# A graph kernel on one core: each selection of the gather stages moved from ahead of its neighbour's lift to the head of its own slot

## The reference, cut to what matters

```python
mean = jax.ops.segment_sum(h, dst, N) / degc
mean_sq = jax.ops.segment_sum(h * h, dst, N) / degc
std = jnp.sqrt(jax.nn.relu(mean_sq - mean * mean) + EPS_VAR)
mx = jax.ops.segment_max(h, dst, N)
mn = jax.ops.segment_min(h, dst, N)
...
out = jnp.concatenate([x, out], axis=-1) @ W_post + b_post
return out @ W_lin + b_lin
```

## Time and profile before

| what | us |
| --- | --- |
| median of 3 runs | 2146.79 |
| lowest and highest of them | 2123.44, 2160.79 |
| the profiled execution's own time | 2106.36 |
| its span, first to last instruction | 2104.6 |
| gather stage of layer 0 in the span | about 636 to 1250 |
| gather stage of layer 1 in the span | about 1362 to 1982 |
| TensorE's mean granted clock | 0.863 |

### The profile page before, as it was taken

The page is one execution under the profiler, slowest core; times in us unless marked ns, Lnnn a source line. Parts: engine busy times, 40 slices in busy tenths (PEclk is TensorE's granted clock), DMA queues, the critical chain, the costliest instruction groups (busy, mean ns, idle before and its releaser), DMA issues.

```text
span 2104.6 us, 30157 instructions
## 1 busy us (share of the span) xinstructions
PE 1443.8 (69%) x11250; PEld 1041.9 (50%) x11250; DVE 1423.3 (68%) x2879; ACT 502.3 (24%) x1074; POOL 804.5 (38%) x831
## 2 busy tenths in 40 slices
PE   0267777666974777877777865636777887787564
PEld 0156777655972444545554542424444554455432
DVE  7899999783425866666666754766655776676457
ACT  3357777500112111111111110310111111111101
POOL 4400000014006455556655624065545555565230
PEclk9879888886996988989988987978888998898876
DMA  5323333322443555555656532344555565565320
GB/s 119 94 110 140 140 140 140 125 87 93 161 139 98 178 171 192 178 186 184 200 167 197 184 113 63 92 141 161 176 181 176 187 201 182 170 219 170 139 63 25
DMA packets 126252, 309.57 MB, mean 147 GB/s; under 512 B 21744, under 2 KB 73408, under 8 KB 125742
## 3 DMA queue, kind: packets, MB, share of 16 engines
q1 hardware_dynamic: 75216, 145.00, 19.7%
q10 hardware_dynamic: 23470, 105.20, 14.2%
q0 software_dynamic: 27440, 57.77, 10.0%
HBM read 167.18 MB, written 140.75 MB: 146 GB/s over the span
## 4 chain that ended last, share of the span: by engine, by line
DVE 34%; PE 32%; issue 14%; another core or an unknown queue 12%; DMA 3%; ACT 2%; POOL 2%; ACTq 1%; DVEq 0%; POOLq 0%
PE ps L1190 16%; PE ps L1305 6%; DVE accs L2246 5%; DVE scanned L2275 4%; DVE accs L2228 4%; DVE scanned L1769 3%; DVE scanned L1766 3%; DVE scanned L1775 3%; PE ps L1317 2%; PE ps L1215 2%; PE ps L1405 1%; DVE S L1742 1%; DMA A<-counts 1%; ACT Y L756 1%
## 5 line engine op out<-in xcount | busy, mean ns | idle before, releaser
L1129 POOL DMA_INDIRECT scanned<-table,rest_idx x688 | 675.2, 981 | 712.1 <-DMA rest_history<-scanned 248.1
L1190 PE MATMUL ps<-big,A 125*128 125x128 bf16 (+1 forms) x7500 | 756.0, 257 | 60.9 <-issue 49.4
L1190 PEld LDWEIGHTS ps<-big,A 125*128 125x128 bf16 x7500 | 622.9, 103 | 190.9 <-issue 83.4
L1305 PE MATMUL ps<-S,big 126*128 126x500 bf16 (+1 forms) x1050 | 276.2, 406 | 251.7 <-DVE accs L2246 171.0
L2246 DVE TENSOR_TENSOR accs<-accs,ps 128x1000 f32<-128x1000 f32 (+1 forms) x154 | 166.7, 1083 | 342.7 <-remote 257.1
L2275 DVE SCALAR_TENSOR_TENSOR scanned<-scanned,rest_neg 128x256 f32<-128x256 f32 x688 | 331.7, 482 | 40.6 <-issue 7.6
L1305 PEld LDWEIGHTS ps<-S,big 126*128 126x128 bf16 x1050 | 101.1, 106 | 371.3 <-DVE accs L2246 187.5
L1215 PE MATMUL ps<-scanned 128*128 128x150 bf16 x1050 | 115.6, 252 | 76.3 <-DVE scanned L1775 75.4
L2228 DVE TENSOR_TENSOR accs<-accs,ps 128x1000 f32<-128x1000 f32 (+1 forms) x154 | 165.9, 1077 | 1.8 <-DVE sums_t L1883 1.3
L1148 POOL IOTA Y<- 128x784 int32 x1 | 0.8, 786 | 359.9 <-DVEq L2033 359.9
L1215 PEld LDWEIGHTS ps<-scanned 128*128 128x128 bf16 x1050 | 87.2, 132 | 92.7 <-issue 71.2
(11 more groups left out here) (395 smaller groups left out, 1410.0 us busy)
## 6 DMA issues: line engine op xcount, KB each, us to landing
rest_history<-scanned SPq DMA_DIRECT2D x172, 512.0 KB
A<-counts ACTq DMA_DIRECT2D x75, 800.0 KB
S<-picks SPq DMA_DIRECT2D x60, 640.0 KB
picks<-S ACTq DMA_DIRECT2D x25, 800.0 KB
counts<-A ACTq DMA_DIRECT2D x25, 800.0 KB
scanned<-table,rest_idx POOLq DMA_INDIRECT x688
table<-Y SPq DMA_DIRECT2D x10, 320.0 KB, 2.6
S<-picks SPq DMA_DIRECT2D x10, 160.0 KB
```

What stands on the lines that cost most here:

```text
L1129: nc.gpsimd.indirect_dma_start(out=lanes[:, r, s, 0:F], out_offset=None, in_=tables[1 + l], in_offset=bass.IndirectOffsetOnAxis(ap=rest_id ...
L1190: m = nc.tensor.matmul(acc[:, bank, 0:width], A[0:NB, slot, a, :], XS[0:NB, a, c, 0:width], start=a == 0 and c == 0, stop=a == NT - 1 and ...
L1305: m = nc.tensor.matmul(ps[:, bank + h, 0:len(blocks) * NB], XS[0:NB + 1, a, c, 0:F], pick[0:NB + 1, part % RING, 0:len(blocks), a % PART, ...
```

## The change

The selection of a slot is issued at the head of that slot. Before, the first one was issued ahead of the loop, and in each slot the next slot's selection was issued ahead of the lift of the current one.

```diff
-                select(l, 0)
                 for s in range(NSLOT):
-                    if s + 1 < NSLOT:
-                        select(l, s + 1)
+                    select(l, s)
                     fold(s)
                     if s - 2 in AT_FRONT:
                         use_operands(l, AT_FRONT[s - 2])
```

## The result

Timed side by side on one chip, the changed kernel took 2163.32 us (median of 4 runs, 2155.39 to 2175.61) and the kernel before 2135.11 us (4 runs, 2110.9 to 2160.79): a ratio of 1.022, with a 95% interval of 1.013 to 1.032. Executions of one kernel spread by a few per cent, and every ratio here leaves out those over 1.5% above the fastest of their kernel, while the medians are over all runs, so a ratio is not the quotient of the two medians beside it (1.013 here). The profiled execution after took 2155.39 us, with a span of 2153.6 us and a mean granted clock of 0.854; before it was 2106.36, 2104.6 and 0.863.

A forecast was written before the change was run, and what follows sets the result against it. No engine was taken as full; the gather stages wait for late TensorE signals. Terms of +2 (clean slots), +12 (after late signals) and -2 (slots 0 to 5) sum to +12 us: 2146.79 becomes 2159 us, range 2106 to 2177.

The forecast's parts named there:

- The wait at the selection: TensorE's idle before the selections that `take_low` ended, 171.0 us, should fall to near nothing.
- rival A: Wait at the selection is a true limit; the chain restarts sooner after late signals: -87 us, 2060 us, chance 0.15.
- The chain inside a slot: Selection start to lift takes 2.72 us, bare by 0.13 or 0.30 us; at most 19.6 us for both layers.
- How many slots pay it: Of 96 slots up to 86 follow a late signal; the ten left pay 0.2 us each, +2 us.
- After a late signal: The next lift comes 0.27 us later after each of 43 late signals, at the low clock: +12 us.
- Where the signals strike: `take_low` should still wait some 40 times for "remote", near 257 us; such waits before `take_top` would contradict this.
- B: Rival: late signals strike the selection too, 1.9 us each, 82 us on top of 12: 2241 us, chance 0.20.
- slots 77 to 90: In slots 78 to 90 the pieces ahead cover a selection and maximum of 125 columns: 0.
- Slots 0 to 5: The lift no longer stands behind a selection waiting for a `take_low`: -1 us a layer.
- The clock: The low clock should last about as long as before; a mean well over 0.863 would speak for a sooner restart.

The follow-up runs named there:

- e1: The kernel before, with the next slot's selection moved from ahead of the current slot's lift to directly behind it: 2131.62 us, ratio 0.987.
- the quiet pair: The kernels before and after, each with three quarters of the row gathers left out: 1787.39 and 1811.77 us, 24.4 us apart.
- e2: The changed kernel, unedited, measured again beside the kernel before: 2167.8 us, ratio 1.004.
- e11: The changed kernel, unedited, measured once more in more rounds beside the kernel before: 2155.0 us, ratio 1.015.
- e10: The changed kernel, with each row gather waiting until the row 14 ahead of it was scanned: 2105.24 us, ratio 0.990 to the kernel before.
- e5_before_quarter_timed: The kernel before with one of four row gathers issued, the other rows scanned as zeros: 1787.39 us, ratio 0.836.

## Why the prediction was right, and where its steps were not

The forecast was 2159 us, 12 above the median, in a range of 2106 to 2177, and a change within 2% was given 0.65. Measured were 2163 us, and +28, +13 and +38 us by the medians of three comparisons, or about +48, +9 and +32 by their ratios: some 30 on the average. The sign held and the range held. The size of the change did not, being over twice the 12, and neither did its split into terms. That 2163 lies 4 us from 2159 is luck: the forecast started from a median of 2146.79 for the kernel before, and beside the changed one it took 2135.11.

**The wait at the selection.** It was to be near nothing, and is (8.4 us of idle in the groups, none of it ended by `take_low`). Behind it there was no 87 us to be had: e1 takes the same wait away without the change's price and gains 24 us, and nothing with the gathers paced. This is rival A at its most.

**The chain inside a slot.** 2.72 us from the start of the selection to the lift, bare by 0.13 us in F and 0.30 in T: measured 2.73 us, 0.15 and 0.31 to 0.33, and 0 in U by the median step. In the pair without late signals, slots 9 to 77 cost 18.2 us where the sum with all slots clean said 19.6. Each duration was in the rows of before, and adding them in the order of their dependence gave the chain's length. That 18.2 is so near 19.6 holds for the sum only: by kinds it is 0.3 in F, 12.8 in T and 5.0 in U, where the prediction had 7.0, 12.6 and 0.

**How many slots pay it.** This is the step that failed, and it failed twice. I took ten of 96 and +2 us, because two slots follow each of 43 late signals. But of those 86 slots many are U slots, lie outside 9 to 77, or follow two late signals: in the trace of before only 53 are F or T slots of 9 to 77, so 43 were left, some +9 us by the prediction's own rule. And the slots behind a late signal do pay. In the three profiles of the kernel after, 51, 60 and 49 F and T slots come one or two behind a wait of over 2 us for a late signal, and in 31, 35 and 29 of them the maximum starts within 0.1 us of the selection's end and the lift within 0.1 us of the maximum's: the chain is bare there too. The times fit: 24.4 us where no signal is late, some 30 on the average where 43 and more are.

**After a late signal.** +0.27 each, 12 us. It can't be read alone. If the other terms are as in the quiet pair, (9 - 24.4) / 43 = -0.36 to (48 - 24.4) / 43 = +0.55 us is left for each, in which a gain and a loss behind a late signal may cancel. A net gain of 2.03 us each (a sooner restart at the full clock) doesn't go with this, nor one of 0.95. Rival A falls with the times: the changed kernel was faster in no comparison.

**Where the signals strike.** `take_low` was to go on waiting for "remote" about 40 times, 257 us. It did 19 times, 62.7 us; 39 times and 209.7 us stand before `take_top`. By the prediction's own test that makes B right, since 77% of the wait moved. Late signals do strike the selection, but the price of 82 us on top is not there: the kernel took 2163 us and not 2241, and the late signals' waits sum to 326, 324 and 326 us in the three profiles after, 36 more than the 290 before. There is one place where the price is seen. In slots 77 to 90, where the prediction had 0 and the quiet pair has +3.5, the stages after are 16.4 us longer than before (18.7 in e2, 14.1 in e11). Of this some 10 is in slot 82, a U slot of 125 columns. In all six stages of three profiles of the kernel after, the step from its predecessor's minimum to its own is 8.5 to 10.1 us, 4.73 and 3.85 before. The timeline of the kernel after shows what stands there:

```profile
1233.17 0.49 PE L1305 MATMUL ps<-S,big 126*128 126x125 bf16 x6
...
1240.26 0.42 DVE L2226 TENSOR_TENSOR accs<-accs,ps 128x250 f32<-128x250 f32 x1 [7.30 <-remote]
...
1240.74 0.39 PE L1317 MATMUL ps<-S,lift 128*128 128x125 bf16 x2 [5.08 <-DVE accs L2226]
```

The selection is recorded to 1233.66, its signal arrives at 1240.26. Before, this selection was made a slot ahead of its maximum, so by the order of the kernel the same lateness would have been covered there; with the gathers paced 14 back it is gone from this slot too (4.62 and 4.65 us in e10). Over the whole stages late selections (241, 242 and 253 us) took the place of most of the late lifts (290 us before; 85, 82 and 73 after); why the sum grows by so little was not shown.

**Slots 0 to 5.** -2 us predicted; -4.3 in the quiet pair over slots 0 to 6, and -8.8, -1.8 and -11.0 in the profiles of after, e2 and e11. The sign was right, and the size too small in most.

**The clock.** It was to be low about as long as before. Over the stages it is 0.88 and 0.87 in both kernels, over the span 0.863 before and 0.854, 0.855 and 0.849 in the three profiles after.

## What to carry to other kernels

Before moving an operation to just ahead of its consumer, add up producer, signal, consumer and signal, and compare it slot by slot with the work that the engine has in between: what is bare is paid in most slots (71 of 96 in the quiet pair), also in many that a larger trouble disturbs (31 of 51 in the kernel after). A long wait of engine X for engine Y beside an equal one of Y for something unnamed is one event; removing the first moved it here and saved little. The lever was the unnamed one: pacing one engine's transfers took 3 to 4% off, more than any order of the others did.

## What the runs showed of the hardware

TensorE's signals arrived up to 13.6 us after the recorded end of the matmul before (17.2 in e11), and they did so only where GpSimd's row gathers were many. With three of four gathers left out, the late signals fell from 54 with 290 us of VectorE's waits to none. Mere load of the DMA engines does not explain it: their busy share was 0.58 and 0.59 in the stages without late signals and 0.53 in those of before (rows below and above). In the rows above, the late signal comes at 1020.69, 2.35 us after the end of the last of a train of gathers (1017.39 + 0.95), with GpSimd stopped until 1025.17. Of the 54 late signals before, 26 came 2.3 to 4.1 us after the start of the last gather, and 28 at most 1.6 us after it; but 87% of the stages' time lies within 4.1 us behind the start of a gather, so it is the runs with fewer gathers that show the link, and not this. The Trainium skill (Perfetto Trace Analysis, on the Tensor Engine Instruction) says that a matmul's reported end is an estimate and that its semaphore follows the acknowledged write. The traces agree that the signal can come long after the recorded end, and can't tell a late semaphore from an end that is recorded too early; what in a gather holds it (its descriptors, its reads or its writes) was not tried, and stays open.

After such a wait TensorE is granted the lower clock for some microseconds, so a wait can cost a little more than its own length. The quiet pair's stages run at 0.96 and 0.97, and with the order of before they take 457 and 449 us instead of 612 and 613 (about 480 was expected).

```profile
638.00:1095.00 457.00, 417.59 (x2816) 288.30 (x2813) 397.48 (x690) 95.44 (x246) 86.60 (x87) 0.96 0.58 196
1212.00:1661.00 449.00, 413.42 (x2804) 285.78 (x2804) 396.88 (x688) 93.26 (x243) 82.42 (x84) 0.97 0.59 202
```

These are the stretches of both stages in e5_before_quarter_timed. 302 us of long waits are gone and the stages are 319 us shorter. How much of the 17 us between them is the clock was not separated.
